# First chunk of the state-space groups: the next masked decays ahead of dt\*x times decay on GpSimd, the next decays ahead of the state's product on TensorE

## The reference

```
proj = u @ W_in.T ; z, x, B, C, dt = split(proj)
x, B, C = silu(causal_conv4(x, B, C) + conv_b)
dt = softplus(dt + dt_bias) ; dA = exp(dt * A)          # 8 heads
S_t = S_(t-1) * dA_t + dt_t * outer(x_t, B_t)           # 64 x 64 a head
y_t = S_t @ C_t
out = ((y + D_param * x) * silu(z)) @ W_out.T
```

## Time and profile before

| | us |
|---|---|
| median of 3 runs | 1778.42 (1778.31 to 1779.15) |
| profiled execution | 1778.96 |
| its span | 1777.2 |
| TensorE busy | 1748.8 (98%) |
| VectorE busy | 1339.1 (75%) |
| ScalarE busy | 942.7 (53%) |
| GpSimd busy | 822.4 (46%) |

### The profile page before, as it was taken

The page is one execution under the profiler, slowest core; times in us unless marked ns, Lnnn a source line. Parts: engine busy times, 40 slices in busy tenths (PEclk is TensorE's granted clock), DMA queues, the critical chain, the costliest instruction groups (busy, mean ns, idle before and its releaser), DMA issues. The chain is left out here.

```text
span 1777.2 us, 35778 instructions
## 1 busy us (share of the span) xinstructions
PE 1748.8 (98%) x13280; PEld 1288.8 (73%) x13280; DVE 1339.1 (75%) x2317; ACT 942.7 (53%) x1421; POOL 822.4 (46%) x565
## 2 busy tenths in 40 slices
PE   7999999999999999999999999999999999999999
PEld 4588888888888844444444444655888888888888
DVE  7988777887766758778778777657887777877655
ACT  7744746557464465545435536334547465474653
POOL 2766436244362426446456456625245263352533
PEclk9999999999999999999999999999999999999999
DMA  8032131111312031211112112012121311112100
GB/s 331 25 90 43 47 89 30 59 42 47 89 36 107 0 104 34 63 36 62 56 37 66 56 36 69 30 66 42 48 43 47 89 41 48 41 48 65 41 24 24
DMA packets 125197, 104.49 MB, mean 59 GB/s; under 512 B 104001, under 2 KB 104513, under 8 KB 119745
## 3 DMA queue, kind: packets, MB, share of 16 engines
q1 hardware_dynamic: 125120, 103.60, 19.1%
HBM read 49.59 MB, written 25.17 MB: 42 GB/s over the span
## 5 line engine op out<-in xcount | busy, mean ns | idle before, releaser
L504 POOL TENSOR_TENSOR f_hlo<-f_h,f_hhi 128x768 f16<-128x768 f32 x135 | 201.5, 1493 | 598.8 <-ACT f_hhi L687 569.9
L1261 PE MATMUL f_gate_ps<-spare 128*128 128x256 f16 x2688 | 329.8, 272 | 0.2
L1185 PE MATMUL f_down_ps<-wd,f_hhi 128*128 128x256 fp8e4 x1440 | 318.4, 273 | 0.7 <-DVE xa L882 0.7
L1185 PE MATMUL f_down_ps<-wd,f_hlo 128*128 128x256 fp8e4 x1440 | 318.4, 273 | 0.0
L1261 PEld LDWEIGHTS f_gate_ps<-spare 128*128 128x128 fp8e4 x2688 | 254.7, 97 | 45.3 <-issue 1.9
L1261 PE MATMUL f_up_ps<-spare,wu 128*128 128x256 f16 x1792 | 229.9, 273 | 0.1
L1261 PEld LDWEIGHTS f_up_ps<-spare,wu 128*128 128x128 fp8e4 x1792 | 172.8, 98 | 23.3 <-issue 0.7
L882 DVE SCALAR_TENSOR_TENSOR xa<-f_down_ps,out_scale,xa 128x512 f32<-128x512 f32 x195 | 136.3, 742 | 59.4 <-PE f_down_ps L1185 59.1
L1647 POOL TENSOR_TENSOR s_am<-s_tri,s_al 128x512 f16<-128x512 f16 x128 | 155.3, 1243 | 21.4 <-DVE s_al L1919 18.8
L1185 PEld LDWEIGHTS f_down_ps<-wd,f_hhi 128*128 128x128 f16 x1440 | 140.9, 98 | 17.8 <-issue 1.6
L1185 PEld LDWEIGHTS f_down_ps<-wd,f_hlo 128*128 128x128 f16 x1440 | 140.9, 98 | 16.3
(11 more groups left out here) (247 smaller groups left out, 3295.2 us busy)
## 6 DMA issues: line engine op xcount, KB each, us to landing
xa<-res SPq DMA_DIRECT2D x16, 1024.0 KB, 5.2
res<-xa SPq DMA_DIRECT2D x15, 1024.0 KB, 3.9
res<-xa SPq DMA_DIRECT2D x34, 256.0 KB, 2.0
xa<-in_u SPq DMA_DIRECT2D x8, 1024.0 KB, 4.8
xa<-res SPq DMA_DIRECT2D x32, 256.0 KB, 2.7
late<-in_w_gate SPq DMA_DIRECT2D x4, 1024.0 KB, 17.0
spare<-in_w_up SPq DMA_DIRECT2D x3, 1024.0 KB, 8.8
late<-in_w_in SPq DMA_DIRECT2D x1, 2320.0 KB, 8.3
```

Source lines behind the costliest of these rows:

```text
L504: last = nc.gpsimd.tensor_tensor(hlo[:, p, a:b, :], src, hhi[:, p, a:b, :], ALU.subtract)
L1185: last = nc.tensor.matmul(at, part[:, p, kind, m * P:(m + 1) * P], wd[:, weight, p, :], start=(p == 0 and part is hhi and (m == 0 or name ...
L1261: last = nc.tensor.matmul(acc[:, j * HT:(j + 1) * HT], w[:, k, e * P:(e + 1) * P], xop[part][:, o, k, :, :], start=(fresh and (j, k, part) ...
```

## The change

decays_first(g, c) is true for chunk 0 of every group but LAST, and for chunks 0 to 2 of EVE. For such a chunk GpSimd runs masked for chunk c + 1 ahead of the wait for dtx and of dtxe, instead of after it. TensorE leaves chunk_state(g, c) out at the end of the chunk and runs it in chunk c + 1, between chunk_decays and chunk_start. GpSimd gets one wait more in the last chunk of EVE and LAST: for the chunk_state of the chunk before, ahead of the counter dtxe_done.

```diff
+                def decays_first(g, c):
+
+                    return c == 0 and g is not LAST or g is EVE and c < CH - 1
...
                                 nc.gpsimd.tensor_tensor(cd[:, :, :], ecb[:, :, :],
                                                         cc[:, b, cols(c)].unsqueeze(1).to_broadcast([P, H // 2, P]), ALU.mult)\
                                   .then_inc(cd_done, 1)
+                                if decays_first(g, c):
+                                    masked(g, c + 1)
                                 if final(g, c):
+                                    pool.wait_ge(st_done, after(q))
                                     pool.sem_inc(dtxe_done, 1)
                                 else:
                                     pool.wait_ge(dtx_done, after(q + 1))
                                     pool.wait_ge(st_done, after(q))
                                     nc.gpsimd.tensor_tensor(heads(dtxe[:, :]), heads(dtx[:, :]), over(to_end(b, c), HD), ALU.mult)\
                                       .then_inc(dtxe_done, 1)
-                                if g is not LAST and c < CH - 1:
+                                if g is not LAST and c < CH - 1 and not decays_first(g, c):
                                     masked(g, c + 1)
-                                elif front is not None:
+                                elif c == CH - 1 and front is not None:
                                     masked(front, 0)
...
                                     chunk_decays(g, c)
+                                if c and decays_first(g, c - 1):
+                                    chunk_state(g, c - 1)
                                 chunk_start(g, c)
...
-                                chunk_state(g, c)
+                                if not decays_first(g, c):
+                                    chunk_state(g, c)
```

## The result

The changed kernel takes 1781.63 us (median of 22 runs, 1780.91 to 1783.2), the kernel before beside it 1779.17. The ratio is 1.0015, with a 95% interval of 1.0009 to 1.0021: 2.7 us slower by the ratio (1.6 to 3.7), 2.5 by the medians. The profiled execution has a span of 1779.1 against 1777.2.

The account below looks back on a forecast made before the run. TensorE, 98% busy, was taken as the bound, with VectorE's queue deciding at chunk_y of chunk 1. Loop +2.4 and EVE +0.1 gave +2.5 us, forecast 1780.9 against the median 1778.42, range 1777.3 to 1783.8.

Parts of the forecast that it names:

- its opening: TensorE in the state-space part: nine of ten waits for masked decays are touched, at most 4.8 us saved directly.
- step 1: GpSimd, chunk 0: masked decays start about 1.3 us earlier, end near 1012.2 to 1012.4, and TensorE's wait at 1012.78 goes.
- Step 2: TensorE, chunk 0 to 1: state's product starts at 1014.21, chunk_start at 1014.69, 0.52 us earlier.
- Step 3: VectorE: the addition to the state starts 0.81 us later, all of it a new hole with the queue behind it.
- Step 4: chunk_y of chunk 1 waits on dtx with slack 0.1 us or none, so the loop's groups cannot cash the 0.52.
- Step 5: VectorE's taps escape the collision with cd; 0.40 of the 0.81 remains, 6 x 0.40 = +2.4 us in the loop.
- Step 6: EVE: +0.6 for chunk 0 to 1, -0.6 for chunk 1 to 2, +0.1 before LAST; in all +0.1 us.
- A: VectorE's queue from the addition to dtx, chunk 0 to 1, gets nothing back: +5.6 us, 1784.0; chance 0.16.
- B: VectorE's queue recovers all and EVE's chunks cash a little, nothing lost or won: about 1778.0; chance 0.23.
- D: Masked decays still come after 1012.78, so TensorE waits as before: +1.0 us per group, 1784; chance 0.06.
- C: TensorE's waits come off, needing dtx 0.5 us earlier in chunk 1: 4.8 us less, 1773.6; chance 0.05.

Follow-up runs that it names:

- e5: Changed kernel with VectorE's four statistics of the group after next split, two in chunk 0 and two in chunk 1: 1777.67 us, ratio 0.9994 to the kernel before.
- e3: Changed kernel with VectorE's addition to the state moved behind the statistics and softplus start, ahead of the taps: 1776.07 us, ratio 0.9983 to the kernel before.
- e9: Kernel before, with the addition to the state moved behind the statistics and softplus start: 1779.81 us, ratio 1.0004 to the kernel before.
- e6: Kernel before, with VectorE's four statistics split between chunks 0 and 1: 1776.99 us, ratio 0.9992 to the kernel before.
- e7: Changed kernel with the state's product moved into chunk_decays, between the products into turn and those into seg: 1778.00 us, ratio 0.9997 to the kernel before.
- e4: The change in the loop's six groups alone, EVE and LAST as in the kernel before: 1781.62 us, ratio 1.0014 to the kernel before.
- e11: e8 with LAST's softplus on VectorE moved from EVE's chunk 3 to its chunks 1 and 2: 1777.18 us, ratio 0.9990 to the kernel before.
- e8: Changed kernel with the state's product between the two halves of the decays and the statistics split: 1774.67 us, ratio 0.9975 to the kernel before.
- e10: Changed kernel with the state's product between the decays' halves and the addition late, statistics whole: 1774.74 us, ratio 0.9979 to the kernel before.
- e1: Changed kernel with GpSimd's half undone, so only TensorE's product is moved: 1790.72 us, ratio 1.0069 to the kernel before.
- e2: Changed kernel with TensorE's half undone, so only GpSimd's masked decays come first: 1779.51 us, ratio 1.0002 to the kernel before.

## Why the prediction was right

*TensorE's waits (its opening and step 1).* Right: nine go, GpSimd is in time at all of them. The tenth is 4.0, forecast 4.1.

*Step 2, TensorE's order.* The direction was right, the size off. Of the 0.52 saved I forecast all at chunk_start; 0.32 arrived (2.43 to 2.11), and 0.10 of it was lost by project_out. e5 gives the sum: 9.94 is TensorE's pace to chunk_y, 0.3 under the kernel before. The forecast didn't need it in the loop, as VectorE came last. One of its signs did: I had named 0.9 to 1.1 of idle time before chunk_y of chunk 1, and it is 0.64 as printed (10.65 - 9.94 = 0.71).

*Step 3, the hole.* The addition is 0.91 later, not 0.81: the product starts 1.53 after the decays, not 1.43. VectorE's printed idle time before it is 1.11, where I had 0.8 to 1.0. The mechanism is shown by e3 and e5: TensorE's order stays, only what stands behind the addition on VectorE is taken from there, and they run about 5.5 and 3.5 us under the changed kernel, while the same edits in the kernel before bring nothing clear (e9, e6).

*Step 4, no slack.* Right, and the centre of it. All seven chunk_y of chunk 1 wait for dtx now.

*Step 5, what comes back.* 0.40 forecast, 0.41 measured. The hole was 0.10 larger and yet cost nothing more, since L1884 ends with cd whenever it comes into it, and cd had not moved (4.58 behind TensorE's point, before 4.57). e7 shows how fine this is: a shift of 0.05 against cd lies between 0.19 and 1.28 for the same instruction.

*Step 6, EVE.* +0.65 for chunk 0 to 1 (0.6 forecast), -0.30 where I had -0.6, and +0.18 to LAST where I had +0.1. The 0.65 is partly luck. The collision of the taps with cd that I put at 0.55 cost 0.88 (3.20 in place of 2.32), and two things that I had not counted took it back: the large product lx took 1.67 in place of 1.90, and L1884 had no collision, 0.19 in place of 0.39.

```profile
1085.74 3.20 DVE L1869 SCALAR_TENSOR_TENSOR s_xc<-s_xpad,late,s_xc 128x512 f32<-128x512 f32 x3
1087.10 1.30 POOL L1674 TENSOR_TENSOR s_cd<-s_ecb,s_cc 128x512 f32<-128x512 f32 x1 [3.28 <-ACT s_ecb L1778]
1089.25 1.67 DVE L1946 TENSOR_TENSOR s_lx<-s_lx,late 128x1024 f32<-128x1024 f32 x1
```

In chunks 2 and 3 TensorE's order takes 0.3 of each saving, which is the term I left out. EVE and LAST's start then lose 0.5 by the trace and not 0.1; e4 says that the time can't tell. In the profiled execution the shorter stretch at the lower clock (-0.68) hid it. So the loop's 2.5 is what the forecast got right by its mechanism; that the total agrees as closely is luck. That EVE's saving is given back at LAST was right about the wait; e11 shows that beyond it other waits lie ready.

*Rivals.* A's condition (nothing comes back) did not arise, nor did B's (the whole queue recovers): the small instruction did not slip through beside cd, and dtx came 0.41 later. No wait was left for D. C needed dtx earlier; e8 and e10 make that so, and reach 4.4 and 3.7 of its 4.8.

Still open is why the new order costs TensorE 0.3. The steps from seg to the product and from the product to chunk_start are 0.97 and 0.58, where 0.88 (seg to chunk_start) and 0.48 (product to the 64 wide decays) stood. That this is the change of width was argued and is not shown; e7 changes the order of widths and takes as long to chunk_start, and gets back only the 0.1 of the step to project_out.

## What to carry to other kernels

When a wait on the busiest engine goes, look for the next thing that it would wait for, and at its slack in the same trace: here 0.1 us, and 0.52 could not be cashed. A product moved behind other work is late for its reader, and in an engine's ordered queue everything behind that reader is late with it; so move the reader back too (e3) or shorten what stands behind it (e5). The change that lost 2.7 us gains 3.0 with the one edit of e3, and 4.4 with the product one step earlier and the statistics split (e8). e11 adds a warning: with one wait removed, two others appeared behind it, and the work that was moved met GpSimd in its new place.

## What the runs showed of the hardware

Small VectorE instructions can pay for what is left of a GpSimd instruction beside them: a 32 wide one took 0.64 (the changed kernel), 0.82, 0.97 (e11) or 1.28 (e7) in place of 0.17 to 0.19 when it fell beside a GpSimd instruction of 1.0 to 1.3. Three of the four ended within 0.05 of GpSimd's: at 1020.41 against 1020.37, 1089.42 against 1089.37, and in e7 1019.44 against 1019.39. So the price of a collision depends on which instruction is hit and when, not only on how much work it has, and a shift of a few hundredths of a microsecond can move it by 1 us.

The stretch at the lower clock behind the wait before LAST has two lengths in these profiles, 3.4 and about 6.8 us, and they do not go with the kernel's order: 3.4 in the changed kernel, e1, e5, e6, e7 and e10, 6.8 in the kernel before, e2, e3, e4, e8 and e9. From LAST's decays to its first chunk_y it makes 9.14 to 9.20 in the first six and 9.87 to 10.48 in the others. e11 has no such wait and takes 8.97, but has its two stretches elsewhere. Whether one kernel changes between the lengths from execution to execution is not shown, as each has one profile. Up to 1.3 us hangs on it, so one profile each is not enough to compare spans to better than that.
